# A two-network graph kernel: relu and residual addition on GpSimd, final statistics on VectorE one unit later

## The chip, the cores and the metric

The kernel runs on one core of one Trainium2 chip. The time is the device time of one execution in microseconds (us).

## What is computed

The input is x, [128 graphs, 64 nodes, 384 features], and an adjacency matrix of 64 x 64 for each graph. Two graph networks run one after the other, each with two layers, each followed by a residual addition and a normalisation without gain:

```python
x = _layernorm(x + _L0_gnn_ref(x, adj, ...), axis=-1)     # first network
x = _layernorm(x + _L1_gnn_ref(x, adj, ...), axis=-1)     # second network
```

The change touches only the second network. One layer of it is

```python
a = jax.nn.softmax(jnp.einsum('bid,bjd->bij', h, h) / temper, axis=-1)
delta = a * adjacency_matrix
attn = delta / (jnp.sum(delta, axis=-1, keepdims=True) + 1e-10)
ctx = (attn * upper) @ (h @ wl.T + b_l) + diag(attn) * (h @ ws.T + b_s) + (attn * lower) @ (h @ wr.T + b_r)
o = (ctx - mean) / jnp.sqrt(var + LN_EPS) * g + beta
h = jax.nn.relu(o)
```

and `_layernorm` is `(x - m) / jnp.sqrt(v + 1e-5)` over the 384 features.

## The kernel before

The 8192 nodes are worked through in tiles of 128 nodes (two graphs). Four tiles (NT = 4, 512 nodes) are a **stream**, and a pass holds two streams, so a network takes 8 passes. A pass has four **units**, in this order: unit 0 is layer 0 of stream 0, unit 1 layer 0 of stream 1, unit 2 layer 1 of stream 0, unit 3 layer 1 of stream 1. All engines have programs of their own with the order of the work written out by hand; semaphores are the only thing between them, and each engine runs strictly in its order. Products are made in split precision: each operand has a high part and a low rest, and three products are summed.

TensorE's order for one unit (`one_pass` of the tensor program): the fold that completes the scores (L1130, L1133); twelve value jobs j = 0 to 11, three sides for each of four tiles, nine products each (`values`, L1157), with transposes between them (L1114, L1141); the scores of the next unit (L119); then the four contexts of this unit (`contexts`, L1170, six products each). Values and contexts go into four PSUM banks in turn, so that job j can only start once job j - 4 has been read. For sides 0 and 1 ScalarE first writes the bias into the bank (`seed`, L1256), and TensorE waits for that; for side 2 TensorE itself waits for the bank.

After a value job ScalarE copies its high part (`value_hi`, L1262) and VectorE subtracts it for the rest (`biased_value`, L1494, or L1498 for side 2), which frees the bank. VectorE copies the contexts into z and takes their statistics (`contexts_out`, L1532 and L1535), and computes the variance (`variances`, L1541 to L1551). GpSimd takes the root (`roots`, L1398), VectorE the offset (`deviations`, L1555), and ScalarE normalises z (`normalise`, L1276), all in the course of the next unit. In VectorE's program `go_on(i, unit)` therefore finishes unit and works on unit + 1 as far as its contexts: value rests 0 to 2, the offset of unit, then `up_to_contexts` of unit + 1, which begins with the probabilities (L1510) and goes on with rests 3 to 11, the rests of the probabilities (L1515), the transposes of the input for the next unit where that is of layer 0 (`flip_block`, L1478, and `turn_lo`, L1468), and the diagonal's sum (`own_probability`, L1520), for which GpSimd has masked the exponentials (`diagonal`, L1394).

For units of layer 1 (units 2 and 3) the output of the network has still to be finished. GpSimd multiplies by the gain and adds the shift (`gain_and_shift`, L1407 and L1409), one tile after the other, with the diagonal of the next unit after the second tile. VectorE adds the residual with the relu in one instruction for each tile (`add_residual`, L1575), tiles 0 and 1 before value rest 11 and tiles 2 and 3 after it, takes the final statistics (`final_stats`, L1581) and the final variance (`final_var`, to L1590), and only then copies the contexts. GpSimd takes the final root at the end of its unit (`final_roots`, L1402), VectorE the final offset after its context copies (L1594). GpSimd normalises (`final_normalise`, L1414) one unit later, at the start of its next unit: stream 0's output in its unit 3, stream 1's in unit 0 of the next pass. SyncE stores the result (L1092). z of a stream is written again by the context copies of its next unit of layer 0, which wait for this store (`stored`). Also on GpSimd: three masks for each stream and pass from the transposed adjacency (`masks`, L1383), which need the adjacency load of that pass (L1061) and the own probability of that stream's last unit.

SyncE's order for a pass: for each stream the load of the residual (L1075, which waits until that stream's sums of the pass before are done) and of the next pass's input (L1056); then for each stream the adjacency load and the store of the output. The last unit of all is done in a shorter way (`end`): GpSimd gains and shifts one tile (LAST_GT = 1) and VectorE three (L1561, L1565), ScalarE and VectorE share the last normalisation.

Of the kernel before, what the change touches and what calls it, by code (L numbers as in the profile page):

```python
# [7 lines left out]
ALU = mybir.AluOpType  # L8
# [924 lines left out]
def softmax_layers(nc, ctx, sh, gated, x1, adj_t, w_nbr_t, table, out):  # L933
# [26 lines left out]
    with ExitStack() as block_ctx:  # L960
# [45 lines left out]
        stage_in = [sem(f"stage_in{n}") for n in range(SIDES)]  # L1006
        upper_split, split = sem("upper_split"), sem("split")
        x_copied = [sem(f"x_copied{s}") for s in range(STREAMS)]
        power_set = sem("power_set")
        keep_ready = [sem(f"keep_ready{s}") for s in range(STREAMS)]  # L1010
        work_full, work_free = sem("work_full"), sh.bank_free
        part_copied, folded = sem("part_copied"), sh.folded
# [35 lines left out]
        def _(sp):  # L1048
# [23 lines left out]
            def one_pass(i, last):  # L1072
                for s in range(STREAMS):
                    wait(sp, summed, i * (STREAMS * NT) + (s + 1 - STREAMS) * NT)
                    sp.dma_start(x_res[s][:], x_v[i, s]).then_inc(x_copied[s], 16)  # L1075
                    if not last:
                        sp.wait_ge(turned, nth(i, s, KO, KO - 1))
                        load_x(i + 1, s)
                for s in range(STREAMS):
                    if not last:  # L1080
                        sp.wait_ge(keep_ready[s], i + 1)
                        load_adj(i + 1, s)
                    if last and s == STREAMS - 1:

                        half = NT // 2
                        sp.wait_ge(out_ready, i * (STREAMS * NT) + NT * s + half)
                        sp.dma_start(out_v[i, s][:, 0:half], z[s][:, 0:half, 0:H]).then_inc(stored[s], 16)
                        sp.wait_ge(last_ready, half)
                        sp.dma_start(out_v[i, s][:, half:], z[s][:, half:, 0:H]).then_inc(stored[s], 16)
                    else:  # L1090
                        sp.wait_ge(out_ready, i * (STREAMS * NT) + NT * (s + 1))
                        sp.dma_start(out_v[i, s], z[s][:, :, 0:H]).then_inc(stored[s], 16)  # L1092
# [110 lines left out]
        def _(act):  # L1203
# [110 lines left out]
            def one_pass(i, last, first=False):  # L1314

                for unit in range(UNITS):
# [9 lines left out]
                        second_half(i, unit + 1, not (last and unit == UNITS - 2), first and unit == 0)  # L1326
                    else:
                        normalise(i, unit, range(LAST_GT))
                    if last and unit >= STREAMS:
                        final_normalise(i, unit - STREAMS, tiles=NT if more else NT // 2)  # L1330

            act.wait_ge(sh.part_set, 1)
            act.wait_ge(sh.next_small, 16 * 7)
# [33 lines left out]
        def _(pool):  # L1367
# [36 lines left out]
            def gain_and_shift(i, s, t):  # L1404
# [3 lines left out]
                pool.wait_ge(gained, done)  # L1408
                nc.gpsimd.tensor_tensor(z[s][:, t, 0:H], z[s][:, t, 0:H], shift[:], ALU.add).then_inc(scaled, 1)  # L1409

            def final_normalise(s):

                for t in range(NT):
                    nc.gpsimd.tensor_scalar(z[s][:, t, 0:H], z[s][:, t, 0:H], frstd[s][:, t:t + 1],  # L1414
                                            foffset[s][:, t:t + 1], ALU.mult, ALU.add).then_inc(out_ready, 1)

            def one_pass(i, last, first=False):

                for unit in range(UNITS):
                    layer, s = divmod(unit, STREAMS)  # L1420
                    more = not (last and unit == UNITS - 1)
                    roots(i, unit)
                    if first and unit == 0:
                        gated_final_roots(1)
                    if unit == 0 and not first:
                        final_normalise(1)
                    if unit == UNITS - 1 and not last:
                        final_normalise(0)
                    if layer == 1:
                        for t in range(NT if more else LAST_GT):  # L1430
                            gain_and_shift(i, s, t)
                            if t == 1:
                                diagonal(i, unit + 1)
                    elif more:
                        diagonal(i, unit + 1)
                    if first and unit == 0:
                        weight_lo(2)
                    if layer == 1:
                        final_roots(i, s)
                    if not last and unit % STREAMS == 1:  # L1440
                        masks(i + 1, unit // STREAMS)

            pool.wait_ge(sh.next_split, SIDES)
            masks(0, 0, first=True)
# [16 lines left out]
        def _(dve):  # L1461
# [139 lines left out]
                    nc.vector.tensor_scalar(z[s][:, t, 0:H], z[s][:, t, 0:H], frstd[s][:, t:t + 1], foffset[s][:, t:t + 1],  # L1601
                                            ALU.mult, ALU.add).then_inc(last_ready, 1)

            def up_to_contexts(i, unit, last, s):

                more = not (last and unit == UNITS - 1)
                flip_next = more and layer_of(unit + 1) == 0
# [5 lines left out]
                        flip_block(i, unit + 1, j - 3)  # L1613
                probabilities_lo(i, unit)
                biased_value(i, unit, 6)
                biased_value(i, unit, 7)
                if flip_next:
                    turn_lo(i, unit + 1, 0)
# [8 lines left out]
                    turn_lo(i, unit + 1, 2)  # L1627
                biased_value(i, unit, 10)
                own_probability(i, unit)
                if s is not None:  # L1630
                    add_residual(i, s, (0, 1))
                biased_value(i, unit, 11)
                if s is not None:
                    add_residual(i, s, (2, 3))
                    final_stats(i, s)
                    final_var(i, s)
                contexts_out(i, unit)
                if s is not None:
                    final_offset(i, s)

            def begin(i, unit):
                variances(i, unit)
# [3 lines left out]
            def go_on(i, unit, last=False, first=False):  # L1646
# [6 lines left out]
                deviations(i, unit)  # L1653
                if first:
                    gated.final_offset()
                up_to_contexts(i, unit + 1, last, s if layer == 1 else None)

            def upper_layer(i, last):
                go_on(i, 1, last)
# [11 lines left out]
            def end(i, s):  # L1671
                unit = UNITS - 1
                variances(i, unit)
                deviations(i, unit)
                last_gain_and_shift(s)
                add_residual(i, s, range(NT), LAST_GT)
                final_stats(i, s)
                final_var(i, s)
# [90 lines left out]
```

## Time and profile before

| | |
|---|---|
| median of 3 runs | 1717.54 us (1716.96 to 1718.06) |
| the profiled execution, own time | 1716.51 us |
| its span in the trace | 1714.9 us |
| TensorE matmuls busy | 1667.0 us, 97% of the span |
| TensorE weight loads busy | 1579.3 us, 92% |
| VectorE busy | 1267.7 us, 74% |
| ScalarE busy | 948.4 us, 55% |
| GpSimd busy | 614.6 us, 36% |
| granted TensorE clock, mean | 0.993 of full speed |

The span is the time from the first to the last instruction of the profiled execution; some 1.6 us of its own time lie around it. The first network ends and the second begins between 840 and 870 us. The second network's passes take 104.2 us each, units of layer 0 some 25 us and those ahead of which TensorE transposes z some 27.

### The profile page before, as it was taken

What the parts mean: (1) busy time and instruction counts of PE and PEld (TensorE: products, weight loads), DVE (VectorE), ACT (ScalarE), POOL (GpSimd) and SP (SyncE); (2) the same over time, 40 slices, a digit from 0 to 9 for tenths busy, and PEclk for the clock granted to TensorE, in tenths of its full rate; (3) what the DMA queues carried; (4) which work ended last, traced back from release to release, by engine and by line L of the source; (5) the groups of instructions that cost most, each with busy time, mean ns of one, the idle gap of its engine ahead of it and who ended that gap; (6) DMA issues with size and microseconds to landing.
All of it is one profiled execution on the core that took longest, in us unless ns stands there. A gap on an engine that the chain in (4) does not pass through costs nothing.

```text
span 1714.9 us, 29860 instructions
## 1 busy us (share of the span) xinstructions
PE 1667.0 (97%) x9664; PEld 1579.3 (92%) x9664; DVE 1267.7 (74%) x2785; ACT 948.4 (55%) x1985; POOL 614.6 (36%) x658
## 2 busy tenths in 40 slices
PE   7999999999999999999989999999999999999994
PEld 6989989899898889889889999999999999999994
DVE  4587685867859578695876877769687696877866
ACT  4545455464554645546556665655655656656653
POOL 5143252432424233243522523525143351523503
PEclk9999999999999999999999999999999999999997
DMA  7015012020300203003013040300304003030101
GB/s 230 1 32 157 6 48 75 24 92 6 104 19 24 92 6 116 6 24 93 21 61 96 22 95 0 102 15 22 95 3 114 1 22 96 22 95 0 64 14 37
DMA packets 108015, 92.19 MB, mean 54 GB/s; under 512 B 63280, under 2 KB 101168, under 8 KB 107952
## 3 DMA queue, kind: packets, MB, share of 16 engines
q1 hardware_dynamic: 107952, 91.51, 18.6%
q8 instruction: 20, 0.33, 0.1%
q14 instruction: 43, 0.35, 0.1%
HBM read 66.33 MB, written 25.17 MB: 53 GB/s over the span
## 4 chain that ended last, share of the span: by engine, by line
PE 51%; issue 32%; POOL 10%; DVE 3%; ACT 2%; SPq 1%; DMA 1%; POOLq 0%; ACTq 0%; DVEq 0%
PE b_work L1157 34%; PE b_work L1170 8%; POOL g_qv_lo L621 3%; POOL b_ht L601 3%; PE b_score_ps L119 3%; PE b_work L372 2%; PE b_score_ps L386 1%; PE b_work L396 1%; POOL g_keep_l L616 1%; POOL g_sigma L630 1%; POOL g_a_nat L617 1%; POOL g_frstd L634 1%; PE b_turn L1114 1%; PE b_score_ps L1133 1%; PE b_score_ps L1130 0%
## 5 line engine op out<-in xcount | busy, mean ns | idle before, releaser
L1157 PE MATMUL b_work<-b_w_hi,b_ht 128*128 128x384 f32 x2304 | 607.0, 338 | 8.3 <-ACT b_work L1256 8.3
L1157 PEld LDWEIGHTS b_work<-b_w_hi,b_ht 128*128 128x128 f32 x2304 | 418.6, 188 | 10.0 <-ACT b_work L1256 9.4
L1157 PE MATMUL b_work<-b_w_lo,b_ht 128*128 128x384 f32 x1152 | 385.9, 335 | 0.0
L372 PE MATMUL b_work<-b_ht,b_w_hi 128*128 128x512 f32 x1152 | 357.7, 392 | 9.5 <-DVE b_w_lo L696 9.5
L372 PEld LDWEIGHTS b_work<-b_ht,b_w_hi 128*128 128x128 f32 x1152 | 216.3, 189 | 51.2 <-issue 9.5
L621 POOL TENSOR_TENSOR g_qv_lo<-g_v_full,g_qv_hi 128x384 fp32r<-128x384 f32 x128 | 133.4, 1062 | 361.0 <-ACT g_qv_hi L495 361.0
L372 PE MATMUL b_work<-b_ht,b_w_lo 128*128 128x512 f32 x576 | 225.8, 392 | 0.0
L1494 DVE TENSOR_TENSOR s_v_lo<-b_work,s_v_hi 128x384 fp32r<-128x384 f32 x256 | 139.3, 554 | 116.1 <-ACT s_v_hi L1262 114.5
L1157 PEld LDWEIGHTS b_work<-b_w_lo,b_ht 128*128 128x128 f32 x1152 | 217.1, 188 | 0.0
L728 DVE TENSOR_TENSOR g_qv_lo<-b_work,g_qv_hi 128x512 fp32r<-128x512 f32 x192 | 128.8, 687 | 111.1 <-ACT g_qv_hi L483 109.2
L396 PE MATMUL b_work<-b_w_hi,b_ht 128*128 128x384 f32 x768 | 206.2, 336 | 0.0
L1256 ACT ACTIVATE b_work<-b_bias 128x384 f32<-128x384 f32 x256 | 126.4, 494 | 120.1 <-DVE b_z L1532 82.0
L483 ACT ACTIVATE g_qv_hi<-b_work 128x512 fp32r<-128x512 f32 x192 | 110.7, 592 | 132.0 <-PE b_work L372 132.0
L1262 ACT ACTIVATE s_v_hi<-b_work 128x384 fp32r<-128x384 f32 x256 | 121.9, 490 | 59.0 <-PE b_work L1157 58.6
L386 PE MATMUL b_score_ps<-g_qv_hi,b_ht 128*128 128x256 f32 x768 | 147.0, 285 | 4.6 <-DVE g_qv_lo L728 4.6
L396 PEld LDWEIGHTS b_work<-b_w_hi,b_ht 128*128 128x128 f32 x768 | 139.8, 188 | 1.3
L372 PEld LDWEIGHTS b_work<-b_ht,b_w_lo 128*128 128x128 f32 x576 | 108.7, 189 | 23.1
L396 PE MATMUL b_work<-b_w_lo,b_ht 128*128 128x384 f32 x384 | 128.6, 335 | 0.0
L386 PEld LDWEIGHTS b_score_ps<-g_qv_hi,b_ht 128*128 128x128 f32 x768 | 120.5, 188 | 8.4 <-DVE g_qv_lo L728 7.2
L1398 POOL TENSOR_TENSOR s_rstd<-s_var,s_power 128x4 f32<-128x4 f32 x32 | 32.2, 1008 | 222.9 <-DVE s_var L1551 222.9
L487 ACT ACTIVATE g_prob<-g_score_l 128x512 f32<-128x512 f32 x32 | 20.2, 632 | 164.5 <-DVE g_score_l L740 164.5
L386 PE MATMUL b_score_ps<-g_qv_lo,b_ht 128*128 128x256 f32 x384 | 107.2, 279 | 0.0
(142 smaller groups left out, 3247.6 us busy)
## 6 DMA issues: line engine op xcount, KB each, us to landing
b_x_in<-in_x_t SPq DMA_DIRECT2D x16, 768.0 KB, 7.2
g_x_res<-in_x SPq DMA_DIRECT2D x16, 768.0 KB, 7.5
x<-b_z SPq DMA_DIRECT2D x16, 768.0 KB, 3.9
b_x_in<-x SPq DMA_DIRECT2D x64, 192.0 KB, 6.7
s_x_res<-x SPq DMA_DIRECT2D x16, 768.0 KB, 6.9
out<-b_z SPq DMA_DIRECT2D x15, 768.0 KB, 4.1
b_a_tr<-in_adj_t SPq DMA_DIRECT2D x64, 64.0 KB, 3.4
g_a_nat<-in_adj SPq DMA_DIRECT2D x32, 64.0 KB, 2.4
```

Of the source, the lines that this page charges most:

```text
L119: mm = pe.matmul(score_ps[:, t, :, :], ht[:, k, 0, tile], ht[:, k, :, tile], start=(t % 2 == 0 and k == 0), stop=False, skip_group_check=True)
L372: mm = pe.matmul(bank[:], w, h, start=(n == 0), stop=(n == len(pairs) - 1))
L386: mm = pe.matmul(score_ps[:, t, :, :], h, q, start=(n == 0), stop=(n == len(pairs) - 1))
L396: mm = pe.matmul(bank[:, 0:H], h, w, start=(n == 0), stop=(n == len(pairs) - 1))
L483: nc.scalar.activation(q_hi[:, m, :, d, :], work[use % RING][:], ACT.Copy).then_inc(q_hi_ready, 1)
L621: nc.gpsimd.tensor_tensor(v_lo[:, t, 0:H], v_full[:, t, :], v_hi[:, t, 0:H].bitcast(F32), ALU.subtract).then_inc(v_lo_ready, 1)
L728: op = nc.vector.tensor_tensor(q_lo[:, m, :, d, :], bank, q_hi[:, m, :, d, :].bitcast(F32), ALU.subtract)
L1157: mm = pe.matmul(bank[:, 0:H], h, w, start=(n == 0 and side == 2), stop=(n == len(pairs) - 1), skip_group_check=True)
L1170: mm = pe.matmul(bank[:, 0:HC], p, v, start=(n == 0), stop=(n == len(pairs) - 1))
L1256: nc.scalar.activation(work[(unit * WN + j) % RING][:, 0:H], bias[:, side, layer_of(unit), :], ACT.Copy)\
L1262: nc.scalar.activation(v_hi[:, t, side, 0:H], work[(unit * WN + j) % RING][:, 0:H], ACT.Copy)\
L1494: nc.vector.tensor_tensor(v_lo[:, t, side, 0:H], bank[:, 0:H], v_hi[:, t, side, 0:H].bitcast(F32), ALU.subtract).then_inc(work_free, 1)
```

## The change

In the second network, the relu and the addition of the residual go from VectorE to GpSimd (`residual_rows`): for each tile GpSimd multiplies by the gain, adds the shift, takes the maximum with 0 and adds the residual, with the tiles interleaved so that most waits are for something issued two instructions before. The final statistics and variance of stream 0 go into `go_on` of unit 3 and those of stream 1 into `go_on` of unit 0 of the next pass, on VectorE between the offset and the probabilities; the final offset goes behind value rest 6 of the same unit. GpSimd takes the final root right behind the root of that unit, waits for the final offset, then masks the diagonal, normalises stream 0 or 1 and, in unit 3, goes on with the rows of stream 1. The diagonal stands ahead of the gain and shift instead of after the second tile. The masks of stream 1 move from GpSimd's unit 3 to its unit 2, behind the rows of stream 0. SyncE issues both adjacency loads ahead of both stores. At the very end stream 0's statistics come between the last offset and the gain of the last unit, its offset behind that, and ScalarE does both last normalisations after its one tile.

```diff
@@ SyncE
-                for s in range(STREAMS):
-                    if not last:
+                if not last:
+                    for s in range(STREAMS):
                         sp.wait_ge(keep_ready[s], i + 1)
                         load_adj(i + 1, s)
+                for s in range(STREAMS):
                     if last and s == STREAMS - 1:
@@ ScalarE, one_pass
-                    if last and unit >= STREAMS:
-                        final_normalise(i, unit - STREAMS, tiles=NT if more else NT // 2)
+                    if not more:
+                        final_normalise(i, 0, tiles=NT)
+                        final_normalise(i, 1, tiles=NT // 2)
@@ GpSimd
+            def residual_rows(i, s):
+
+                def done(t):
+                    return i * (STREAMS * NT) + s * NT + t + 1
+
+                for t in range(NT + 1):
+                    if t < NT:
+                        pool.wait_ge(normed, done(t))
+                        if t > 0:
+                            pool.wait_ge(scaled, done(t - 1))
+                        nc.gpsimd.tensor_tensor(z[s][:, t, 0:H], z[s][:, t, 0:H], gain[:], ALU.mult).then_inc(gained, 1)
+                    if t > 0:
+
+                        nc.gpsimd.tensor_scalar(z[s][:, t - 1, 0:H], z[s][:, t - 1, 0:H], 0.0, None, ALU.max)                            .then_inc(lifted, 1)
+                    if t < NT:
+                        pool.wait_ge(gained, done(t))
+                        nc.gpsimd.tensor_tensor(z[s][:, t, 0:H], z[s][:, t, 0:H], shift[:], ALU.add).then_inc(scaled, 1)
+                    if t > 0:
+                        pool.wait_ge(x_copied[s], 16 * (i + 1))
+                        pool.wait_ge(lifted, done(t - 1))
+                        if t == NT - 1:
+                            pool.wait_ge(scaled, done(t))
+                        nc.gpsimd.tensor_tensor(z[s][:, t - 1, 0:H], z[s][:, t - 1, 0:H], x_res[s][:, t - 1, :], ALU.add)                            .then_inc(summed, 1)
@@ GpSimd, one_pass
                     if unit == 0 and not first:
+                        final_roots(i - 1, 1)
+                        pool.wait_ge(foffset_ready, i * STREAMS)
+                        diagonal(i, unit + 1)
                         final_normalise(1)
-                    if unit == UNITS - 1 and not last:
+                    elif unit == UNITS - 1 and more:
+                        final_roots(i, 0)
+                        pool.wait_ge(foffset_ready, i * STREAMS + 1)
+                        diagonal(i, unit + 1)
                         final_normalise(0)
-                    if layer == 1:
-                        for t in range(NT if more else LAST_GT):
-                            gain_and_shift(i, s, t)
-                            if t == 1:
-                                diagonal(i, unit + 1)
                     elif more:
                         diagonal(i, unit + 1)
+                    else:
+                        final_roots(i, 0)
+                    if layer == 1:
+                        if more:
+                            residual_rows(i, s)
+                        else:
+                            gain_and_shift(i, s, 0)
                     if first and unit == 0:
                         weight_lo(2)
-                    if layer == 1:
+                    if not more:
                         final_roots(i, s)
-                    if not last and unit % STREAMS == 1:
-                        masks(i + 1, unit // STREAMS)
+                    if not last and unit in (1, 2):
+                        masks(i + 1, unit - 1)
@@ VectorE, up_to_contexts
                 biased_value(i, unit, 6)
+                if finals is not None:
+                    final_offset(*finals)
                 biased_value(i, unit, 7)
...
                 own_probability(i, unit)
-                if s is not None:
-                    add_residual(i, s, (0, 1))
                 biased_value(i, unit, 11)
-                if s is not None:
-                    add_residual(i, s, (2, 3))
-                    final_stats(i, s)
-                    final_var(i, s)
                 contexts_out(i, unit)
-                if s is not None:
-                    final_offset(i, s)
@@ VectorE, go_on
-                up_to_contexts(i, unit + 1, last, s if layer == 1 else None)
+                finals = None
+                if unit == UNITS - 1:
+                    finals = i, 0
+                elif unit == 0 and not first:
+                    finals = i - 1, 1
+                if finals is not None:
+                    final_stats(*finals)
+                    final_var(*finals)
+                up_to_contexts(i, unit + 1, last, finals)
@@ VectorE, end
                 deviations(i, unit)
+                final_stats(i, 0)
+                final_var(i, 0)
                 last_gain_and_shift(s)
+                final_offset(i, 0)
                 add_residual(i, s, range(NT), LAST_GT)
```

## Rows read from the trace of the kernel before

**Rows 1.** page of the profile, busy time by engine

```profile
PE 1667.0 (97%) x9664; PEld 1579.3 (92%) x9664; DVE 1267.7 (74%) x2785; ACT 948.4 (55%) x1985; POOL 614.6 (36%) x658
```

**Rows 2.** waits of TensorE over the span: line, releaser, us in total, times, longest

```profile
PE b_work L1157 <- ACT b_work L1256: 8.3, 3, 3.3
```

**Rows 3.** timeline of TensorE in a pass: start us, us, engine, line, operation, tiles

```profile
1276.72 0.56 PE L1133 MATMUL b_score_ps<-b_eye_r,b_part 128*128 128x128 f32 x4
1277.11 0.40 PE L1157 MATMUL b_work<-b_w_hi,b_ht 128*128 128x384 f32 x1
...
1295.89 1.59 PE L119 MATMUL b_score_ps<-b_ht 128*128 128x256 f32 x12
...
1301.80 0.56 PE L1133 MATMUL b_score_ps<-b_eye_r,b_part 128*128 128x128 f32 x4
1302.30 0.44 PE L1157 MATMUL b_work<-b_w_hi,b_ht 128*128 128x384 f32 x1
```

**Rows 4.** timeline of ScalarE in the same pass

```profile
1276.51 0.50 ACT L1256 ACTIVATE b_work<-b_bias 128x384 f32<-128x384 f32 x1 [3.31 <-DVE b_z L1532]
...
1301.76 0.50 ACT L1256 ACTIVATE b_work<-b_bias 128x384 f32<-128x384 f32 x1 [3.47 <-DVE b_z L1532]
```

**Rows 5.** timeline of VectorE in the same pass

```profile
1258.49 1.30 DVE L1510 TENSOR_TENSOR b_turn<-b_turn,s_keep 128x512 f32<-128x512 f32 x2 [0.50 <-PE b_turn L1141]
...
1270.44 0.67 DVE L1520 TENSOR_REDUCE s_own<-s_expo 128x4 f32<-128x512 f32 x1
...
1273.37 1.93 DVE L1581 BATCH_NORM_STATS2 s_fstats<-b_z 128x6 f32<-128x384 f32 x4
...
1275.86 0.62 DVE L1532 SCALAR_TENSOR_TENSOR b_z<-s_v_own,s_own,b_work 128x385 f32<-128x385 f32 x1
...
1282.53 0.40 DVE L1555 SCALAR_TENSOR_TENSOR s_offset<-s_mv,s_rstd 128x4 f32<-128x4 f32 x1
1282.85 1.28 DVE L1510 TENSOR_TENSOR b_turn<-b_turn,s_keep 128x512 f32<-128x512 f32 x2
...
1289.10 0.54 DVE L1494 TENSOR_TENSOR s_v_lo<-b_work,s_v_hi 128x384 fp32r<-128x384 f32 x1
...
1295.53 0.68 DVE L1520 TENSOR_REDUCE s_own<-s_expo 128x4 f32<-128x512 f32 x1
```

**Rows 6.** timeline of GpSimd in the same pass

```profile
1246.18 3.79 POOL L1383 TENSOR_TENSOR s_keep<-b_a_tr,b_const 128x512 f32<-128x512 f32 x3 [13.25 <-DVE s_own L1520]
...
1260.26 1.02 POOL L1409 TENSOR_TENSOR b_z<-b_z,b_shift 128x384 f32<-128x384 f32 x1
...
1262.18 0.86 POOL L1409 TENSOR_TENSOR b_z<-b_z,b_shift 128x384 f32<-128x384 f32 x1
1263.01 1.30 POOL L1394 TENSOR_TENSOR s_expo<-s_expo,s_keep 128x512 f32<-128x512 f32 x1
...
1282.25 2.60 POOL L1414 TENSOR_SCALAR b_z<-b_z,s_frstd,s_foffset 128x384 f32<-128x384 f32 x4
...
1306.60 1.01 POOL L1398 TENSOR_TENSOR s_rstd<-s_var,s_power 128x4 f32<-128x4 f32 x1 [0.73 <-DVE s_var L1551]
```

**Rows 7.** timelines of VectorE and of GpSimd where the networks meet

```profile
890.42 1.25 DVE L821 SCALAR_TENSOR_TENSOR g_foffset<-g_fmv,g_frstd 128x4 f32<-128x4 f32 x1
...
890.36 1.29 POOL L1394 TENSOR_TENSOR s_expo<-s_expo,s_keep 128x512 f32<-128x512 f32 x1
```

**Rows 8.** the stored output as a tile, its landings

```profile
DMA to landing us min/median/max: 2.5/4.1/5.6
```

**Rows 9.** timeline of SyncE, last DMAs of the pass

```profile
1320.60 2.37 SPq L1061 DMA_DIRECT2D b_a_tr<-in_adj_t  x2
```

**Rows 10.** timelines of TensorE and of VectorE at the end

```profile
1687.41 0.34 PE L1170 MATMUL b_work<-s_v_hi,s_prob_hi 128*128 128x386 f32 x1
...
1692.45 0.62 DVE L1532 SCALAR_TENSOR_TENSOR b_z<-s_v_own,s_own,b_work 128x385 f32<-128x385 f32 x1
...
1698.87 0.17 DVE L1555 SCALAR_TENSOR_TENSOR s_offset<-s_mv,s_rstd 128x4 f32<-128x4 f32 x1 [1.12 <-POOL s_rstd L1398]
```

More of the change, by code:

```diff
@@ L1008, in softmax_layers @@
         x_copied = [sem(f"x_copied{s}") for s in range(STREAMS)]
-        power_set = sem("power_set")
+        power_set, lifted = sem("power_set"), sem("lifted")
         keep_ready = [sem(f"keep_ready{s}") for s in range(STREAMS)]
@@ L1602, in final_normalise, with up_to_contexts @@
                                             ALU.mult, ALU.add).then_inc(last_ready, 1)
-            def up_to_contexts(i, unit, last, s):
+            def up_to_contexts(i, unit, last, finals):
                 more = not (last and unit == UNITS - 1)
```

## The prediction

> **What bounds the kernel now.** I read the page first: TensorE is busy for 97% of the span, the others far less [rows 1]. Then the waits of TensorE: over the whole span its value products waited 8.3 us for ScalarE, three times [rows 2]; the same view of 840 to 1000 us alone gives the same row, so all three stand where the two networks meet. In a steady pass of the second network TensorE waits for nothing that this view shows, so a gain there has to come from something smaller, and a loss from a new wait.
>
> I call a "stretch" the time of one unit on TensorE, from its first value product. One pass has four of about 26 us; the other engines run one unit's leftovers in the next stretch. In the pass shown, stretch 3 ends and stretch 0 starts at 1277.11, and stretch 1 starts at 1302.30 [rows 3]. At the first boundary the fold product begins 0.39 before the value product, at the second 0.50. There ScalarE's seed began at 1301.76 and took 0.50 [rows 4], because VectorE's first context copy came late behind residual and statistics: TensorE lost 0.11 us. At 1277.11 the same seed, at 1276.51, came just in time.
>
> **What it removes.** In stretches 3 and 0 VectorE no longer adds the residual (4 x 0.55 us) or takes statistics before the context copies: 2.49 us from the first bn_stats to the first copy [rows 5]. So both seeds come in time. Worth: 7 x 0.11 = 0.8 us.
>
> **What it adds on VectorE.** The same 2.49 us now stand between the offset of the layer norm (L1555) and the probabilities (L1510), in stretches 0 and 1. Who waits: L1510, the value rests j = 3 and later, and through the four banks ScalarE's seed 7, without which TensorE can't begin value 7. That product begins 63 products after the stretch does. 108 products take 1295.89 - 1277.11 = 18.78, so 10.95 later: 1288.06 in stretch 0, and 1302.19 + 10.95 = 1313.14 in stretch 1, the 0.11 being gone [rows 3]. From the start of L1555 to the seed's end: offset 0.1, statistics 2.5, probabilities 1.2, value rest 0.55, seed 0.5, hand-overs 0.1 = 4.95 us [rows 4, 5]. In stretch 0 L1555 starts at 1282.5 as now (the value product 2 before it sets this), so the seed is there at 1287.5: it fits with 0.6 to spare, and costs nothing. If that cover goes, each us costs 7 us. The final offset, 0.15 us, is hidden likewise.
>
> **What it adds on GpSimd.** Per stream and pass four relus and four additions, 32 instructions for two streams with the eight multiplications and eight additions that were there. Price: three two-operand instructions start within 2.75 us, the last of the three gaps being 0.83 [rows 6]; twelve at 0.93 are 11.2. No row shows a relu. Nearest is the final normalisation, also one tensor in and one out: four in 2.60, so 0.65 each [rows 6]; I take 0.65, with bounds of 0 and 1.0 (a two-operand instruction). Four: 2.6. Waits on an instruction just issued: 0.1. And VectorE's three small two-operand operations for the variance fall among these rows. The rows show what such a meeting does: a [128 x 4] offset took 1.25 us when it met a GpSimd instruction begun 0.06 before [rows 7], and 0.40 where it met the normalisation [rows 5, 6]. I give GpSimd 0.3 for it; VectorE's own part is hidden, as it has to wait for GpSimd's root anyway. Sum for one stream: 14.2 us.
>
> The Trainium skill (SBUF — State Buffer, section "SBUF: two separate sides") says of this that VectorE with two SBUF inputs and GpSimd exclude each other for a whole instruction. By that rule VectorE loses up to 3 x 0.95 there; the sum stays as it is, for the reason given.
>
> In stretch 3 this fits: the order is diagonal at 1258.5 (with L1510), rows to 1274, masks of the next pass (3.8, moved here from the end of stretch 0, waiting for the own probability of unit 3, done at 1271.1 [rows 5]) to 1278. The variance of unit 3 is ready near 1279 (copies begun 2.4 before 1275.86, and 5.3 on). Queued behind that wait is the root, not late.
>
> In stretch 0 it doesn't fit. GpSimd now waits for the final offset before the diagonal, the normalisation and the rows. When is it? L1510 starts at 1282.5 + 0.1 + 2.5 = 1285.1 instead of 1282.85. From there to value rest 6 it is 6.25 now [rows 5], 1.0 of it idle; 5.2 without. Then rest 6 (0.5) and the offset (0.15): 1290.9. Diagonal 1.3: 1292.2 (VectorE wants it at 1295.53 [rows 5]). Normalisation 2.6: 1294.8. Rows 14.2: 1309.0. Root of unit 0, 1.0: **1310.0, where before it was 1307.6** [rows 6]. L1555 then starts at 1310.0, not 1307.6, seed 7 is there at 1314.95, and value 7 was due at 1313.14: **TensorE stands 1.8 us**. It happens in stretch 1 of passes 1 to 7: 7 x 1.8 = 12.6 us.
>
> **Queues and stores.** SP issues the same DMAs. The store of stream 0 moves from 1284.9 to 1294.8; landing took 2.5 to 5.6, median 4.1 [rows 8]: 1298.9. VectorE's first copy of unit 0, possible at 1298.6 (2.7 behind the scores of 1295.89), waits 0.3 for it, and a copy begun by 1301.0 is soon enough for the seed of 1302.19 (copy 0.6, seed 0.5): 0. The second copy gate, on stream 1's store, is the same a stretch later. Stream 1's store goes out near 1322.3 (L1555 at 1310.0, then the 8.4 from 1282.5 to 1290.9 again, diagonal and normalisation 3.9) instead of 1310.2, and lands at 1326.4, with unit 1's first copy due at 1325.2 + 1.8 = 1327.0; behind it are both residual loads, both input loads (now up to 1320.6) and the adjacency loads, 2.37 for one stream [rows 9] and now for both: issued by 1338, landed by 1342. The masks want them at 1246.18 + 104.2 = 1350.4 [rows 6], flips and residual later still: 0. Both adjacency loads now stand ahead of the first store, on waits met a pass ago: 0.
>
> **The tail.** The last contexts start at 1687.41 on TensorE; VectorE's copies start at 1692.45, held up by the old statistics [rows 10]. Free of them they end with TensorE's products, 3.8 us earlier. After the offset (1698.87 now) 2.5 us of statistics come in: 1.3 gained, less some 0.4 because stream 0's root on GpSimd now meets VectorE's gain operations (as in rows 7). -0.9.
>
> **Sum.** -0.8 + 12.6 - 0.9 = +10.9 us. The profiled execution took 1716.5, so 1727.4; its time is 1.0 under the median of the three runs, so against the median 1717.5 + 10.9 = 1728.4, said as 1728. About 0.2%, 3.4 us, is what a measurement of this kernel can tell from no change.
>
> **Rivals.**
> *A: the rows clear in time (not slower).* Place: GpSimd between 1294.8 and 1309.0. There is no stand if one stream's rows take 12.4 us or less. Twelve at the fastest spacing, 0.83, and a relu with one operation at half of the two-operation row, 0.32, give 11.3. Then only the gains are left: 1717.5 - 1.7 = 1715.8, no measurable change. For it: one gap in three is 0.83. Against: the other two are not, and they belong to the same code. 0.13.
> *B: the relu alone is cheap.* If one operation costs half of the row with two, 0.33 each, the rows take 12.9, the stand is 0.5, 7 of them 3.5: 1719.3, within the noise. Against: the one-input row of this kernel costs 0.65. 0.12. The Trainium skill (GPSIMD Engine Reference, section "Engine selection") says that one-input work on GpSimd is roughly at line rate; with its 1.03 cycles an element at 1.2 GHz, 384 elements are an estimated 0.33 us. The trace's 0.65 for a one-input instruction doesn't agree.
> *C: VectorE's chain is the one that breaks.* Place: statistics ahead of the probabilities, stretches 0 and 1. It decides once they take 0.6 more than 2.5, say through hand-overs with ScalarE. At 1.1 more, stretch 0 loses 0.5 and stretch 1 another 1.1 (GpSimd's own lateness included): 7 x 1.6 = 11 on top, 1739. For it: the margin is one instruction wide. Against: the row has 2.49 for just this chain, and no ScalarE work in it. 0.12.
> *D: the store holds unit 0's copies.* A landing later than 1301.0 would make TensorE wait at 1302.19. But the stretch then starts later and GpSimd doesn't, so the 1.8 shrinks by as much: no price of its own under 8 us of landing. Inside the forecast.
>
> **How the numbers follow.** Forecast, a stand of 1 to 3 us in each of seven passes: 0.58. A 0.13, B 0.12, C 0.12, something unseen that gains over 3.4 us 0.05. Bounds of the relu: at 1.0 the stand is 3.2, or 1738; at 0 none, 1715.8. The forecast's own range is 1723 to 1736. For 8 in 10 it reaches to A and B below, and leaves most of C out above: 1715.5 to 1737. Faster 0.05, same A and B 0.25, slower 0.58 + 0.12 = 0.70.
>
> **What would show it.** Right: in the waits of TensorE a new group of seven waits of 1 to 3 us of value products for ScalarE's seeds, one in each pass but the first, in stretch 1; GpSimd's root of unit 0 starting right behind the rows, with no idle time; VectorE idle before L1555 there, released by GpSimd's root; the 0.11 gone; last contexts 3.8 us sooner behind TensorE's. Wrong: root of unit 0 preceded by idle time (A), a relu of 0.3 (B), waits in stretch 0 too (C), or passes of 104.2 us as now.

## The result, and the profile after

The changed kernel takes 1769.8 us (median of 4 runs, 1767.3 to 1771.8) against 1717.6 for the kernel before: a ratio of 1.0305, 95% interval 1.0289 to 1.0321. It is slower, as forecast, but by 52 us where 11 were forecast, far outside the range. The profiled execution took 1770.1 us, its span is 1768.5.

The page of the changed kernel, busy times (as [rows 1]):

```profile
PE 1689.0 (96%) x9664; PEld 1598.6 (90%) x9664; DVE 1255.4 (71%) x2725; ACT 949.9 (54%) x1985; POOL 737.0 (42%) x778
```

GpSimd's busy time rose by 122 us and still is less than half of the span. TensorE's *busy* time rose by 22 us with the same 9664 matmuls, so besides standing it also ran slower somewhere.

The waits of TensorE, and those of GpSimd and VectorE (as [rows 2]):

```profile
PE b_work L1158 <- ACT b_work L1257: 40.3, 15, 3.7
...
POOL s_expo L1396 <- DVE s_foffset L1628: 58.4, 14, 4.7
...
DVE s_offset L1589 <- POOL s_rstd L1400: 30.8, 8, 4.4
DVE s_v_lo L1528 <- issue: 25.2, 5, 5.5
```

Of TensorE's 15 waits for the seed (8.3 us in three before) seven are those foretold. The line of VectorE that ends in "issue" was not: five times it stood idle with nothing to wait for that the profile shows.

A "stand" is a time in which TensorE has nothing to do and waits, here for ScalarE's seed. The first value products of units 0, 1 and 2 of one pass on TensorE, each of the last two followed by a product that came behind a stand (as [rows 3]):

```profile
964.66 0.39 PE L1158 MATMUL b_work<-b_w_hi,b_ht 128*128 128x384 f32 x1
...
989.76 0.39 PE L1158 MATMUL b_work<-b_w_hi,b_ht 128*128 128x384 f32 x1
...
1004.23 0.69 PE L1158 MATMUL b_work<-b_w_hi,b_ht 128*128 128x384 f32 x1 [3.31 <-ACT b_work L1257]
...
1021.33 0.39 PE L1158 MATMUL b_work<-b_w_hi,b_ht 128*128 128x384 f32 x1
...
1030.40 0.44 PE L1158 MATMUL b_work<-b_w_hi,b_ht 128*128 128x384 f32 x1 [2.14 <-ACT b_work L1257]
```

Read in every pass, these marks give the length of each stretch:

| us | stretch 0 | 1 | 2 | 3 |
|---|---|---|---|---|
| before | 25.2 | 26.5 | 26.9 | 25.6 |
| after, passes 1 to 7 | 25.1 | 31.6 to 33.1 | 28.3 to 31.0 (passes 1 to 5), 26.9 (6, 7) | 25.6 |

Stretch 1 lost 40.3 us over seven passes, of them 24.3 standing (3.31 to 3.69 each). Stretch 2 lost 14.9 over five, of them 8.9 standing (1.12 to 2.29). Stretch 0 gained 0.6, the tail 1.1. That is all but 0.2 of the 53.6 us between the spans; these 0.2 lie ahead of pass 1.

**Stretch 1.** GpSimd's timeline ahead of the stand (as [rows 6]):

```profile
978.36 1.29 POOL L1396 TENSOR_TENSOR s_expo<-s_expo,s_keep 128x512 f32<-128x512 f32 x1 [4.56 <-DVE s_foffset L1628]
979.64 2.60 POOL L1440 TENSOR_SCALAR b_z<-b_z,s_frstd,s_foffset 128x384 f32<-128x384 f32 x4
982.21 1.02 POOL L1423 TENSOR_TENSOR b_z<-b_z,b_gain 128x384 f32<-128x384 f32 x1
...
985.30 1.17 POOL L1426 TENSOR_SCALAR b_z<-b_z 128x384 f32<-128x384 f32 x1
...
987.26 1.01 POOL L1435 TENSOR_TENSOR b_z<-b_z,s_x_res 128x384 f32<-128x384 f32 x1
...
998.27 1.04 POOL L1400 TENSOR_TENSOR s_rstd<-s_var,s_power 128x4 f32<-128x4 f32 x1
```

The rows of stream 1 run from 982.21 to 998.27, 16.1 us; the relu (L1426) takes 1.17 where 0.65 was assumed. The root starts right behind them. VectorE waits for it (as [rows 5]):

```profile
990.71 0.67 DVE L1575 SCALAR_TENSOR_TENSOR s_total<-s_exp_sum,b_z 128x4 f32<-128x4 f32 x1
...
991.60 0.61 DVE L1581 SCALAR_TENSOR_TENSOR s_total<-s_total 128x4 f32<-128x4 f32 x1
992.24 0.79 DVE L1585 TENSOR_TENSOR s_var<-s_mv,s_total 128x4 f32<-128x4 f32 x1
...
999.33 0.16 DVE L1589 SCALAR_TENSOR_TENSOR s_offset<-s_mv,s_rstd 128x4 f32<-128x4 f32 x1 [4.06 <-POOL s_rstd L1400]
```

**The clock.** TensorE's busy time and granted clock (column "PEclk") in windows around the two stands:

```profile
core 0: us, PE busy (x) PEld busy (x) DVE busy (x) ACT busy (x) POOL busy (x), PEclk, DMA share, GB/s
1000.00:1004.20 4.20, 0.92 (x6) 0.60 (x4) 4.12 (x14) 3.30 (x8) 1.01 (x1) 1.00 0.00 0
1004.20:1007.70 3.50, 3.47 (x11) 3.47 (x12) 2.20 (x5) 1.93 (x5) 0.91 (x1) 0.51 0.00 0
1007.70:1012.00 4.30, 4.30 (x31) 4.23 (x30) 1.81 (x3) 3.06 (x6) 2.96 (x5) 1.00 0.08 30
...
1031.40:1035.00 3.60, 3.60 (x13) 3.60 (x12) 1.70 (x4) 3.60 (x8) 0.00 (x0) 0.53 0.00 0
```

Behind each of these two stands the granted clock is 0.5 for some 3.4 us, which is the lower level of 1.2 GHz. In stretch 1 of passes 2, 4 and 6 it lasts twice as long. In stretch 2 of passes 2 and 4, behind stands of 1.19 and 1.12 us, it stays at 1.00. In the kernel before it is 1.00 in the same places.

**Stretch 2.** VectorE, and SyncE's queue beside it (as [rows 9]):

```profile
1023.69 0.17 DVE L1520 TENSOR_SCALAR s_exp_bias<-s_row_max 128x4 f32<-128x4 f32 x1
1029.26 1.02 DVE L1528 TENSOR_TENSOR s_v_lo<-b_work,s_v_hi 128x384 fp32r<-128x384 f32 x2 [5.40 <-issue]
...
1010.69 0.41 SPq L1093 DMA_DIRECT2D out<-b_z  x1
1011.43 0.39 SPq L1075 DMA_DIRECT2D s_x_res<-x  x1
1012.11 3.52 SPq L1056 DMA_DIRECT2D b_x_in<-x  x4
...
1017.87 4.03 SPq L1056 DMA_DIRECT2D b_x_in<-x  x4
1022.09 4.43 SPq L1061 DMA_DIRECT2D b_a_tr<-in_adj_t  x4
```

At 1023.86 VectorE has reached the end of its loop's body and branches back; nothing starts for 5.4 us. SyncE's loads, behind the now later store of stream 1, lie over that branch; before, the first x load was issued at 999.04, 13 us earlier, and all were over. VectorE's timeline at the same place in the kernel before:

```profile
1018.56 0.17 DVE L1486 TENSOR_SCALAR s_exp_bias<-s_row_max 128x4 f32<-128x4 f32 x1
1021.55 1.02 DVE L1494 TENSOR_TENSOR s_v_lo<-b_work,s_v_hi 128x384 fp32r<-128x384 f32 x2 [2.83 <-ACT s_v_hi L1262]
```

There it idled 2.83 us, put down to ScalarE, and TensorE didn't feel it (stretch 2 is 26.9). The DMA queues in this time, 1018.6 to 1021.6 (packets, MB, share of the DMA engines):

```profile
DMA packets 1, 0.01 MB, mean 3 GB/s; under 512 B 0, under 2 KB 0, under 8 KB 0
...
q14 instruction: 1, 0.01, 1.0%
```

and in the changed kernel, 1023.8 to 1029.4:

```profile
DMA packets 2470, 0.79 MB, mean 141 GB/s; under 512 B 2468, under 2 KB 2468, under 8 KB 2468
...
q1 hardware_dynamic: 2468, 0.77, 86.0%
q14 instruction: 2, 0.02, 1.8%
```

Alone on the engines before was one packet, of the instruction queue. Now there are two, among 2468 others. The trace has a start for each packet, though not the engine that it serves. Before, the instruction packet starts 0.9 us after VectorE's last instruction has ended and ends at 1020.14, and VectorE restarts 1.4 us behind it. In the changed kernel the last of the two starts 2.6 us after VectorE has stopped and ends at 1027.49; VectorE restarts 1.8 us behind it.

### The profile page after: what moved, and what is told of

Its sections match the earlier page's. It is cut to its first block, busy times and chain, and to the rows that moved or that the text cites. A ratio compares the mean times of both kernels' runs of the same rounds, so it can differ in the third digit from the quotient of the medians.

```text
span 1768.5 us, 30025 instructions
## 1 busy us (share of the span) xinstructions
PE 1689.0 (96%) x9664; PEld 1598.6 (90%) x9664; DVE 1255.4 (71%) x2725; ACT 949.9 (54%) x1985; POOL 737.0 (42%) x778
## 4 chain that ended last, share of the span: by engine, by line
issue 36%; PE 36%; POOL 16%; DVE 8%; ACT 2%; SPq 1%; DMA 1%; POOLq 0%; DVEq 0%; ACTq 0%
PE b_work L1158 22%; PE b_work L1171 5%; POOL g_qv_lo L621 3%; POOL b_ht L601 3%; PE b_work L372 2%; PE b_score_ps L119 2%; POOL b_z L1426 2%; DVE s_fstats L1615 2%; POOL b_z L1423 1%; POOL b_z L1440 1%; PE b_score_ps L386 1%; PE b_work L396 1%; POOL g_keep_l L616 1%; POOL g_sigma L630 1%; POOL g_a_nat L617 1%
## 5 line engine op out<-in xcount | busy, mean ns | idle before, releaser
L1158 PE MATMUL b_work<-b_w_hi,b_ht 128*128 128x384 f32 x2304 | 624.3, 346 | 40.3 <-ACT b_work L1257 40.3
L1158 PEld LDWEIGHTS b_work<-b_w_hi,b_ht 128*128 128x128 f32 x2304 | 431.6, 194 | 44.5 <-ACT b_work L1257 44.5
L1158 PE MATMUL b_work<-b_w_lo,b_ht 128*128 128x384 f32 x1152 | 394.1, 342 | 0.0
L1158 PEld LDWEIGHTS b_work<-b_w_lo,b_ht 128*128 128x128 f32 x1152 | 223.8, 194 | 0.0
L396 PE MATMUL b_work<-b_w_hi,b_ht 128*128 128x384 f32 x768 | 206.2, 336 | 0.0
L396 PEld LDWEIGHTS b_work<-b_w_hi,b_ht 128*128 128x128 f32 x768 | 139.7, 188 | 1.2
L396 PE MATMUL b_work<-b_w_lo,b_ht 128*128 128x384 f32 x384 | 128.6, 335 | 0.0
L1566 DVE SCALAR_TENSOR_TENSOR b_z<-s_v_own,s_own,b_work 128x385 f32<-128x385 f32 x128 | 77.3, 604 | 49.3 <-PE b_work L1171 49.3
```

Source lines behind the costliest of these rows:

```text
L396: mm = pe.matmul(bank[:, 0:H], h, w, start=(n == 0), stop=(n == len(pairs) - 1))
L1158: mm = pe.matmul(bank[:, 0:H], h, w, start=(n == 0 and side == 2), stop=(n == len(pairs) - 1), skip_group_check=True)
L1566: nc.vector.scalar_tensor_tensor(z[s][:, t, 0:H + 1], v_own[:, t, :], own[:, t:t + 1], bank[:, 0:H + 1], ALU.mult, ALU.add).then_inc(work_ ...
```

## The experiments

Each is a small edit of one of the two kernels. "Loads later" stands for this edit of SyncE's part, which begins a pass's loads only after VectorE's branch:

```diff
                 for s in range(STREAMS):
+                    if s == 0:
+                        sp.wait_ge(exp_turned, in_layer(i, 2))
                     wait(sp, summed, ...)
```

**1. No relu.** The changed kernel without L1426 and without the wait on it; the relu of the second network is left out.

> Leaves out the relu of the second network's last layer, nothing else of the change. Theory 1 (the relu's price, 1.14 us from start to start instead of my 0.65, makes GpSimd late in stretch 1, and all the rest follows from that lateness): a stream's rows take 16.1 - 4 x 1.14 = 11.5 us, under the 12.4 us from which nothing stands; GpSimd's root of unit 0 starts at its variance or at most 0.5 later, no stand of TensorE behind 1000 us, passes of 104.1 us, 1715 to 1717 us. Rival (the statistics ahead of the probabilities, or the moved masks and loads, stall by themselves): passes stay over 106 us and the time over 1730.

Measured: 1737.8 us, ratio 1.0112 (1.0095 to 1.0129). 32 of the 52 us are gone: stretch 1 is 26.5 in all passes, with rows of 11.7 us. But stretch 2 is 31.4 to 32.4 in passes 1 to 5, worse than with the relu, with this wait of VectorE:

```profile
DVE s_v_lo L1524 <- issue: 32.2, 5, 6.9
```

In pass 1 the store went out at 1008.2 and the loads were issued until 1023.9, over the branch at 1020.4. So the relu explains stretch 1 alone, and there is a second cause.

**2. Four forms of the relu,** one for each tile (maximum with 0; maximum and multiplication by 1; maximum with a column of zeros and addition of one; multiplication and maximum).

> The changed kernel with the relu in four forms, one for each tile: tile 0 one operation (maximum with the immediate 0), tile 1 two operations with immediates (maximum 0, times 1), tile 2 two operations with operands from a column of zeros (maximum, plus 0), tile 3 times 1 and then maximum 0, immediates. If the maximum itself is slow on GpSimd, all four take 1.1 to 1.2 us. If a single operation takes a slower path than two, tile 0 takes 1.17 and the others 0.65, as the final normalisation with its two operations does. If immediates are slow and operands fast, only tile 2 takes 0.65.

Measured: 1776.4 us, a single run. The groups of GpSimd by form, in the order normalisation, column, multiplication first, multiplication second, maximum alone:

```profile
L1450 POOL TENSOR_SCALAR b_z<-b_z,s_frstd,s_foffset 128x384 f32<-128x384 f32 x56 | 36.4, 663 | 0.0
...
L1433 POOL TENSOR_SCALAR b_z<-b_z,s_zeros 128x384 f32<-128x384 f32 x15 | 24.7, 1649 | 0.0
L1435 POOL TENSOR_SCALAR b_z<-b_z 128x384 f32<-128x384 f32 x15 | 22.6, 1509 | 0.0
L1431 POOL TENSOR_SCALAR b_z<-b_z 128x384 f32<-128x384 f32 x15 | 22.5, 1501 | 0.0
...
L1429 POOL TENSOR_SCALAR b_z<-b_z 128x384 f32<-128x384 f32 x15 | 17.7, 1183 | 0.1
```

The plain maximum is the cheapest of them, at 1.18, and each second operation beside it makes it dearer. The normalisation, two operations without a maximum, takes 0.66.

**3. Loads later, in the changed kernel.**

> The changed kernel, with one wait more on SyncE: a pass's burst of loads (residual, input, adjacency) is held until the transposed exponentials of unit 2 are there, about 7 us into stretch 2, behind the point where VectorE's loop branches back. Theory 2 (VectorE's second stand, 4.4 to 5.5 us without a releaser at its loop's end, is its instructions being fetched behind this burst): VectorE's idle time there falls under 3.2 us, as in the kernel before, TensorE's stand in stretch 2 (1.1 to 2.3 us in five passes) goes, and with it the half-speed clock of 3.4 us behind it, worth 1.7 each: stretches 2 of 27.0 us, 13 to 16 us less than the changed kernel, about 1755. Rival (the idle time comes from the loop or from GpSimd's lateness, whatever the queues do): stays 4.4 to 5.5 and the time stays within 3 us of 1770, or rises where the masks wait for the later loads.

Measured: 1753.4 us, ratio 1.0209 (1.0192 to 1.0226). Stretch 2 is 26.9 in every pass and VectorE's "issue" wait is gone (it idles 2.8 to 3.0 there); stretch 1 keeps its stands of 3.35 to 3.74.

**4. Loads over the branch, in the kernel before.**

```diff
                 for s in range(STREAMS):
+                    if s == 0:
+                        sp.wait_ge(turned, nth(i, 2, KO, 2))
```

> The kernel before, with one wait more on SyncE: the burst of loads of a pass is held until TensorE's third transpose of unit 2, so that it lies over VectorE's branch as it does in the changed kernel. Nothing of the change is in it. Theory 2: VectorE idles 4.4 to 5.5 us at its branch with no releaser shown, TensorE stands 1 to 2.3 us in stretch 2 of up to six passes, with 1.7 us of half-speed clock behind each: 15 to 25 us slower than before, 1733 to 1743. Rival (a late burst by itself does nothing): 1717 to 1718.

Measured: 1729.2 us, ratio 1.0070 (1.0053 to 1.0086): less than expected. The loss is where it should be, in stretch 2 of passes 1 to 5 (28.8 to 29.0), with nothing of the change in the kernel. The wait of VectorE is there:

```profile
DVE s_v_lo L1496 <- issue: 24.6, 5, 5.0
```

What is missing in the profiled execution is the fall of the clock (the windows are as above, the number ahead of the last two is the granted clock):

```profile
1018.00:1023.00 5.00, 5.00 (x31) 4.96 (x30) 1.04 (x5) 2.68 (x11) 1.01 (x1) 1.00 0.89 147
1025.10:1028.50 3.40, 3.40 (x19) 3.40 (x20) 2.19 (x5) 3.02 (x6) 0.00 (x0) 1.00 0.00 0
```

These stands are 1.57 to 1.78 us, and behind them the clock stays at 1.00. The profiled execution is the shortest of the four, 1726.8 us at a mean granted clock of 0.993; the others took 1728.6 to 1731.9 at 0.990 and 0.991, so the clock may have fallen in them, which no trace shows.

**5. No relu and loads later.**

> The changed kernel with both suspects taken out: no relu on GpSimd (output differs), and SyncE begins a pass's loads only when the exponentials of unit 2 are turned, behind VectorE's branch. If relu and load burst are the whole loss, as the single edits say, neither stretch 1 nor stretch 2 has a stand: stretches 25.1, 26.5, 26.9, 25.6, passes of 104.1, and 1715 to 1718 us. If the two are not the whole (the roots one unit later, or the final statistics in another place, cost something too), stands of over 1 us remain somewhere and the time stays over 1721.

Measured: 1715.9 us, ratio 0.9990 (0.9981 to 1.0). No stand is left in passes 1 to 7; the two causes are the whole loss.

**6. A cheap step in the relu's place, loads later:** `tensor_scalar(z, z, 1.0, 0.0, ALU.mult, ALU.add)`; the relu is left out.

> The changed kernel with the loads behind the branch and, in place of the relu, a multiplication by 1 and addition of 0 of the same tile (output differs: no relu). It should take about 0.66 us, as the final normalisation does: the price that the prediction put on the relu. Then stream 1's rows take about 14.2 us instead of 16.1, the root comes 1.9 us earlier, TensorE stands 1.5 to 1.9 us in stretch 1 of seven passes, and the time is 1727 to 1730 us if short stands cost no clock (1728 was predicted), up to 1745 if the clock falls behind these stands too. If the step takes over 1 us like the relu, the time is that of the changed kernel with loads later, 1753.

Measured: 1723.5 us, ratio 1.0034 (1.0021 to 1.0047). With immediates the step takes 0.51 or 0.52, not 0.66:

```profile
984.30 1.01 POOL L1425 TENSOR_TENSOR b_z<-b_z,b_gain 128x384 f32<-128x384 f32 x1
...
996.24 0.52 POOL L1428 TENSOR_SCALAR b_z<-b_z 128x384 f32<-128x384 f32 x1
...
997.73 1.02 POOL L1402 TENSOR_TENSOR s_rstd<-s_var,s_power 128x4 f32<-128x4 f32 x1
```

Rows of 13.4 us, stands of 0.67 to 1.06 in seven passes, clock at 1.00 behind them. The prediction had a stand begin at rows of 12.4: with 11.7, 13.4 and 16.1 us that would be none, 1.0 and 3.7; measured none, 0.8 and 3.5.

**7. Control: loads later, in the kernel before.**

> Control: the kernel before with the same added wait of SyncE, loads of a pass begun only when the exponentials of unit 2 are turned. If the wait itself costs or gains nothing, 1716 to 1719 us and passes of 104.2. If later loads delay the masks or the next pass's first tiles, stretch 3 or 0 grows and the time is 1722 or more; if the kernel before already lost something to its loads, it comes out under 1715.

Measured: 1717.6 us, ratio 1.0001 (0.9991 to 1.0010). The added wait costs and gains nothing.

**8. The complete change, GpSimd's wait filled and loads later.** In a pass's last unit the rows of stream 1 begin right behind the final root, and the wait for the offset goes behind the shift of their second tile:

```diff
                         final_roots(i, 0)
-                        pool.wait_ge(foffset_ready, i * STREAMS + 1)
-                        diagonal(i, unit + 1)
-                        final_normalise(0)
...
+                    if t == 1 and between is not None:
+                        between()
```

where `between` holds the three lines taken out.

> The changed kernel complete, relu on GpSimd at 1.17 us, with the loads behind VectorE's branch and with GpSimd's order in stream 1's unit changed: the rows begin right behind the final root of stream 0, where GpSimd waits some 4.6 us for VectorE's offset, and the wait, the diagonal and the final normalisation (3.9 us) come between the second and the third tile. The root of the next unit should come about 4.5 us earlier than in the changed kernel (near 8.5 us behind the first value product of stretch 1 less 4.5), more than the stand of 3.3 to 3.7 us, so stretch 1 is 26.5 again, the clock stays up, and the time is 1715 to 1718 us: the change at its intended price. If instead the late diagonal holds TensorE's turning of the next unit, or the late normalisation holds the store and the loads, a new stand shows in stretch 0 or 3 and the time is 1720 or more.

Measured: 1716.0 us, ratio 0.9991 (0.9982 to 1.0), relu on GpSimd included. GpSimd no longer waits at 974.9:

```profile
974.89 1.02 POOL L1425 TENSOR_TENSOR b_z<-b_z,b_gain 128x384 f32<-128x384 f32 x1
...
980.09 1.30 POOL L1398 TENSOR_TENSOR s_expo<-s_expo,s_keep 128x512 f32<-128x512 f32 x1
981.38 2.62 POOL L1444 TENSOR_SCALAR b_z<-b_z,s_frstd,s_foffset 128x384 f32<-128x384 f32 x4
983.97 1.01 POOL L1439 TENSOR_TENSOR b_z<-b_z,s_x_res 128x384 f32<-128x384 f32 x1
...
994.99 1.04 POOL L1402 TENSOR_TENSOR s_rstd<-s_var,s_power 128x4 f32<-128x4 f32 x1
```

The root starts 4.1 us into stretch 1 (990.88) where it had 8.5, VectorE's offset comes at 996.31 without a wait, and the stretches are 25.1, 26.5, 26.9 and 25.6 in all passes from 1 on.

**9. The same without "loads later".**

> The changed kernel complete with GpSimd's wait filled (rows begun behind the final root, diagonal and final normalisation between the second and third tile) but SyncE's loads as the change has them. If the two losses are independent, stretch 1 is 26.5 as with the loads moved, and the load burst, which starts with the store of stream 1 some 3 us earlier than in the changed kernel and so lies like that of the kernel without relu, makes stretch 2 of passes 1 to 5 31 to 32.5: 1735 to 1742 us, not the 1716 of both edits together. If filling the wait also takes the burst off VectorE's branch, 1716 to 1722.

Measured: 1739.3 us, ratio 1.0126 (1.0110 to 1.0143). Stretch 1 is clean, stretch 2 is 31.2 to 32.1 in passes 1 to 5. The two losses are independent: an earlier GpSimd alone leaves the burst over the branch, where VectorE's wait is even longer (up to 6.6 us).

**10 and 11. Which loads?** The kernel before with only its x loads over the branch (edit 4, and the adjacency loads held until the exponentials of unit 2 are turned); and with only its adjacency loads there (`sp.wait_ge(var_ready, nth(i, 1, 1, 0))` ahead of them).

> The kernel before with its x loads (over 3 MB in long rows) begun as in the run that put all loads over VectorE's branch, and the adjacency loads (256 KB in rows under 512 bytes, 4,300 packets and more) only behind it. If bytes make the instruction fetch late, VectorE's wait at the branch stays near 5 us and stretch 2 near 28.9 in passes 1 to 5. If the many small packets of the adjacency do it, the wait is back at 2.8 to 3.1 and stretch 2 at 26.9: 1717 us.

> The kernel before with its x loads where they were and only the adjacency loads put over VectorE's branch: SyncE issues them when the variances of unit 1 are there, about 0.7 us ahead of the branch. If the small packets make the fetch late, VectorE waits 4.5 to 7 us at the branch and stretch 2 is 28.5 to 32 in passes 1 to 5 (1727 to 1745 us). If bytes do it, nothing changes: wait 2.8 to 3.1, stretch 2 26.9, 1717 us.

Measured, one run each: 1724.7 and 1718.8 us. With the x loads VectorE's wait is 4.4 to 4.9 and stretch 2 is 28.3 to 28.8; with the adjacency loads it is 2.9 to 3.1, and stretch 2 is 26.9 or 27.0 in four of the five passes (27.6 in one). So the 3 MB of x are enough to do it. Run 11 tests less than its expectation says: only two of the four adjacency loads, 128 KB, lie over the branch there, 544 packets in VectorE's idle time against 925 to 1105 in run 10. Whether it goes by bytes or by packets is left open: in run 10 too, 4258 of the 4773 packets from 1012 to 1030 us were under 512 bytes, so the expectation's "long rows" were wrong.

## Why the prediction was wrong

**Right.** The direction; the place, in stretch 1 of passes 1 to 7, and the chain from the rows to GpSimd's root, VectorE's L1555 (L1589 after) and seed 7. Counted from the start of stretch 0, 964.66, the offset was there at 13.7 us (13.8 foretold) and the normalisation done at 17.6 (17.7). The 0.11 us at the seed came in passes 1 to 6 (pass 7 had lost nothing there), stretches 0 and 3 were unhurt, the tail gained 1.1 (0.9 foretold). Rival C fell: the statistics ahead of the probabilities cost stretch 0 nothing.

VectorE's three variance operations among GpSimd's rows took 0.67, 0.61 and 0.79 us instead of 0.17, 0.13 and 0.16 outside them. The Trainium skill (SBUF — State Buffer, "SBUF: two separate sides") has GpSimd and a VectorE operation with two SBUF inputs exclude each other for a whole instruction, and this trace agrees; as foretold it was hidden, since VectorE waits for the root behind it.

**Wrong, first: "I take 0.65, with bounds of 0 and 1.0".** The relu takes 1.17, above even the upper bound, which was that of an instruction with twice the input. The rows became 16.1 us instead of 14.2, the stand 3.5 instead of 1.8: 24.3 us over seven passes where 12.6 stood, so 11.7 of the missing 42.7. The nearest row was a normalisation of the same shape and the same instruction form, TENSOR_SCALAR, but another arithmetic operation; runs 2 and 6 show that the operation sets the price (maximum alone 1.18, multiplication and addition 0.52, both with immediates). The Trainium skill (GPSIMD Engine Reference, "Engine selection") has one-input work roughly at line rate; here a maximum takes as long as a two-input addition and a quarter more (1.17 against 0.94), so the rule doesn't hold for it.

**Wrong, second: no price for the clock.** The sum took a stand of TensorE at its own length. In passes 1 to 7 of all runs the granted clock fell to the lower level behind 34 of 36 stands of 2.1 to 4.6 us, and behind none of 22 of up to 2.0 us. The two exceptions, 3.35 us in run 3 and 2.19 in run 2, show that the length alone doesn't decide it; what else does is left open. Stretch 1 lost 15.9 us beside its stands. Run 6 shows the other side: seven stands of 0.8, together 5.8 us, cost 7.9 in all against the stretches without a stand of run 5, 0.3 each beside their length, at a clock of 1.00.

**Wrong, third: "Queues and stores", 0.** The prediction moved the store of stream 1 and the loads behind it some 12 us back and asked only whether each landed in time. It did not ask what else uses the DMA engines then. VectorE's loop branches back once a pass, and packets of an instruction queue pass over the same DMA engines then. With that queue alone VectorE idles 2.8 to 3.1 us there; with the x loads in flight it idles 4.4 to 6.9. This cost 14.9 us with the clock behind it. Runs 3, 4, 7 and 10 show that it hangs on the position of the loads. It also takes the branch: at the end of the loop, in pass 6, VectorE doesn't branch back, and although some 1600 packets of the loads lie over its idle time it idles 2.4 us, as in pass 7 without loads and without a stand of TensorE. The Trainium skill (Runtime: NRT & Kernel Launch, "Instruction fetch mechanics") says that a taken branch out of the engine's small window forces a DMA fetch before execution goes on; that agrees with the packet seen in the trace. The page doesn't say that data delays it; the traces do. At the branch of passes 1 to 5 of all 13 kernels VectorE restarts 1.4 to 1.8 us behind the end of the last instruction packet. What differs is when this packet starts: 0.9 to 1.2 us after VectorE has stopped where no x load is in flight (35 passes), 2.4 to 4.7 us where one is (30 passes). Why it starts late, and that it is VectorE's, is inferred from its place; no record says it. Unrolling the loop, which would take the branch away, wasn't tried.

10.9 + 11.7 + 15.9 + 14.9 = 53.4, against 53.6 between the spans. Put right (run 8), the change is worth about what rival A had, a gain of 1.7: 1716.0 against 1717.3 on the same chip, hardly more than can be measured.

## What to carry to other kernels

Price an operation by a row with the same arithmetic operation, not by one with the same shape; where there is none, let the upper bound lie above the dearest instruction of that size. Where a move delays a transfer, look at what else is on the DMA engines at its new place, the instruction packets at a loop's branch (here VectorE's) among them: to begin the burst after the branch cost nothing in the kernel before (run 7). A stand of TensorE can cost half as much again behind it, here in three passes nearly as much again. First fill the waits of the engine that is late (here 4.6 us of GpSimd's): that gave back the whole loss of stretch 1, and beginning the loads after the branch gave back that of stretch 2.

## What was not expected of the hardware

- A maximum with 0 on GpSimd, [128 x 384] f32, takes 1.17 us; with a second operation 1.50 to 1.65. Multiplication and addition take 0.52 with immediates, 0.66 with column operands.
- At its loop's branch VectorE idles 2.8 to 3.1 us with the instruction queue alone, up to 6.9 beside a load of 3 MB, yet only 2.9 to 3.1 beside 128 KB. It restarts 1.4 to 1.8 us behind the last instruction packet in all cases; it is the packet that starts late.
- In one of seven passes of run 3 the clock stayed at 1.00 behind a stand of 3.35 us, in the other six it fell behind stands of 3.43 to 3.74: the same kernel meets both.
